# Spreading the routing gates over the adapter rows: eight DMAs inside SBUF in place of eight matmuls with a 0/1 matrix

## The chip, the core and the metric

The kernel runs on one core of a Trainium2 chip. The metric is the device time of one execution in microseconds (us), as the median over several executions. The core has a matrix engine (TensorE, PE in the rows), a vector engine (VectorE, DVE), a scalar engine (ScalarE, ACT), a slower general engine (GpSimd, POOL) and a queue engine that issues most transfers (SyncE, SP). ACT can issue transfers too. Sixteen DMA engines carry all transfers.

## What is computed

The input is a batch of 32 images of 64 rows by 1024 values. Two layers are applied, each as "x plus the feed-forward of a conditioned x". Cut to what matters here:

```
u  = conv1d(x) + context bias                  # layer 0, conditioning
x1 = x + u @ W^T + bias + low-rank adapters    # layer 0, feed-forward
v  = per-image 64x64 mixing of x1 + bias       # layer 1, conditioning

scores = v @ Wr^T                              # 64 scores for each of the 2048 rows
top_vals, top_idx = top_k(scores, 16)
G = 0 everywhere, softmax(top_vals) at top_idx # [2048, 64] gates
h = einsum('nd,krd->nkr', v, A)                # 64 adapters of rank 16: 1024 values a row
out = x1 + 2 * einsum('nkr,kdr->nd', h * G[:, :, None], B)
```

The change is in `h * G[:, :, None]`: one gate of an adapter multiplies the 16 values of its rank.

## The kernel before

**Tiling.** The batch is worked in four groups of 8 images (512 rows each; `g` is the group, `TOK` is 512). Each group goes through the convolution, the first feed-forward, the mixing, the scores, the top 16, `h`, and the last product. The weights come as 24 pieces of 128 x 1024 (`pieces`, 512 KB each) that are loaded anew in every group: pieces 0 to 7 for the first feed-forward, 8 to 15 for `h` (A), 16 to 23 for the last product (B).

**Split products.** Every large product is made of three matmuls of 128x128 by 128x512: the factors are split into a rounded part (`_hi`, made by ACT) and the rest (`_lo`, made by DVE), and `product` (lines 794 to 796) adds hi x hi, lo x hi and hi x lo. So each piece costs ACT one copy (line 390), DVE one subtraction (line 572) and PE 24 matmuls. Three pieces are held at a time (`SLOTS`): a piece is split as soon as the piece three before it has been used (`next_piece` on ACT, `split_piece` on DVE), and SP loads the next one into `raw` when a split is done.

**The stage around the change.** `h` is made in eight chunks of 128 rows (8 adapters x 16 ranks), one for each piece 8 to 15; `h_part(c)` on PE writes chunk `c` to PSUM bank `c % 4`. Beside chunks 1 and 2, DVE finds the 16 largest scores and makes `gate`, laid out by row. PE then turns the gates round (line 951, `banks[6]`: 64 adapters x 512 rows). From there, in the kernel before:

- ACT copies the rounded gates to `gate_r` (line 443), DVE puts the rest beside them (line 699);
- PE multiplies them with `expand_r`, a 0/1 matrix that repeats each adapter's gate on 16 rows (`spread`, line 930), two such matmuls in the middle of each of `h_part(3)` to `h_part(6)`, into banks 7 and 5;
- ACT copies each of these from PSUM to `gate_x` (line 452), which has two slots;
- DVE multiplies chunk `c` of `h` with its slot of `gate_x` into the three-slot `ring` (`gated`, line 708); ACT and DVE split the result into `u_hi` and `u_lo` (lines 405 and 582).

**Who waits for whom.** All order is set by semaphores in code that is written out by hand; each engine works strictly in the order of its own program. `h_part(c)` for `c` from 4 on waits until `gated(c - 4)` has freed its bank (line 914, `s_ring`) and until its piece is split (line 800, `s_piece_lo`). The last product, piece `n` from 16 on, waits for its piece and for the two chunks that it reads (line 967). On DVE the order is: `gated` of two chunks, the two rests `u_lo`, then `split_piece(14)`; the same for the next pairs with pieces 15 and 16; then chunk 6 with piece 17 and chunk 7 with piece 18 (lines 711 to 720).

Of the kernel before, what the change touches and what calls it, by code (L numbers as in the profile page):

```python
# [24 lines left out]
F32 = mybir.dt.float32  # L25
F32R = mybir.dt.float32r
# [5 lines left out]
P = 128  # L32
# [19 lines left out]
RING = 24  # L52
LAG = 3
WARM_UP = 12
NEG = -3.0e38


def adaln_ffn_kernel(nc, conv_x, x, taps, pieces, first_consts, hidden_w, later_consts, lora_a, lora_b,
                     starts, wr, expand, spread, out):
    with ExitStack() as ctx:  # L60
# [22 lines left out]
        mixb_bc = sb("mixb_bc", [P, NB, C])  # L83
        agg = sb("agg", [P, NB // 2, C])
        blockdiag = sb("blockdiag", [P, NT, P])
        expand_r = sb("expand_r", [P, L], F32R)
        lora_a_r = sb("lora_a_r", [P, PH, LORA_M], F32R)
        lora_m1 = sb("lora_m1", [P, L], F32R)
        lora_m2 = sb("lora_m2", [P, L], F32R)
# [9 lines left out]
        expd = sb("expd", [P, NT, KR_E])  # L99
        gate = sb("gate", [P, NT, KR_E])  # L100
        stat = sb("stat", [P, 3, NT])
        gate_r = sb("gate_r", [P, TOK], F32R)
        gate_x = sb("gate_x", [P, 2, TOK])

        consts1 = sb("consts1", [P, sum(w for _, w in FIRST)])
        consts2 = sb("consts2", [P, sum(w for _, w in LATER)])
# [18 lines left out]
        mixb, brow, acol, ecol, mixw = (columns(consts2, LATER, n) for n, _ in LATER)  # L125
        mixw = mixw.rearrange("p (k c) -> p k c", c=C)

        agg_part = gate_x[:, :, :].rearrange("p a (b c) -> p (a b) c", c=C)
        lora_a_raw = score_t[:, 0:PH * LORA].rearrange("p (k m) -> p k m", m=LORA)
        wr_raw = blockdiag[:, :, :].rearrange("p t n -> p (t n)").rearrange("p (k m) -> p k m", m=KR_E)  # L130
        w0s = gate[:, 0:2, :].rearrange("p t e -> p (t e)")
# [3 lines left out]
        reached = left[:, 0, 0:2, :].rearrange("p t e -> p (t e)").rearrange("p (n b) -> p n b", b=NB)  # L135
        count = left[:, 0, 2, :].rearrange("p (n b) -> p n b", b=NB)

        expand_stage, lora_b_stage = x1[:, 0, :], x1[:, 1, :]
        diag = x1[0:C, 2, 0:GB * C].rearrange("p (b c) -> p b c", b=GB)

        banks = [ctx.enter_context(nc.psum_tensor(f"bank{i}", [P, HALF], F32)) for i in range(8)]
# [53 lines left out]
        s_gate = sem("s_gate")  # L195
        s_gate_t = sem("s_gate_t")
        s_gate_hi = sem("s_gate_hi")
        s_gate_lo = sem("s_gate_lo")
        s_spread = sem("s_spread")
        s_gate_x = sem("s_gate_x")  # L200
        s_h = sem("s_h")
        s_out = sem("s_out")
        s_stored = sem("s_stored")
# [28 lines left out]
        @block.sync  # L232
        def _(sp):
            def load_piece(n):
                sp.dma_start(raw[:, n % SLOTS, :], pieces[n % PIECES]).then_inc(s_raw[n % SLOTS], 16)

            def load_conv_in(g, t):
                sp.dma_start(conv_in[:, 2 * t:2 * t + 2].rearrange("p b g q -> p (b g q)"),
                             conv_x[bass.ds(g, 1), t].rearrange("a p n -> (a p) n")).then_inc(s_convin[t], 16)

            def load_x(g, t):
                sp.dma_start(x1[:, t, :], x[bass.ds(g, 1), t].rearrange("a p n -> (a p) n")).then_inc(s_x, 16)

            load_conv_in(0, 0)
            load_taps(sp, 2)
            load_taps(sp, 3)
            sp.dma_start(hidden_stage, hidden_w).then_inc(s_first, 16)
            load_conv_in(0, 1)
            load_piece(0)
            sp.dma_start(consts2[:, :], later_consts).then_inc(s_later, 16)  # L250
            load_conv_in(0, 2)
            load_conv_in(0, 3)
            load_piece(1)
            load_piece(2)
            sp.dma_start(lora_a_raw, lora_a).then_inc(s_expand, 16)
            sp.dma_start(starts_i[:, :], starts.to_broadcast([P, 4])).then_inc(s_starts, 16)
            sp.dma_start(lora_b_stage, lora_b).then_inc(s_expand, 16)
            sp.dma_start(wr_raw, wr).then_inc(s_expand, 16)
            sp.dma_start(expand_stage, expand).then_inc(s_expand, 16)
            def group(g, first, last):  # L260
                for n in range(PIECES):

                    sp.wait_ge(s_piece_lo, g * PIECES + n + 1)
                    load_piece(n + SLOTS)
                    if n == 1 and first:


                        sp.wait_ge(s_const_hi, 5)
                        sp.wait_ge(s_const_lo, 3)
                        sp.wait_ge(s_p_ctx_bc, 1)  # L270
                        for t in range(NT):
                            load_x(0, t)
                    if n == 1 and not last:

                        sp.wait_ge(s_conv, g * GB + GB)
                        for t in range(NT):
                            load_conv_in(g + 1, t)
                    if n == 21:
                        store_half(g, 0)
                store_half(g, 1)  # L280
                if not last:

                    sp.wait_ge(s_stored, g * (16 * 2 * NT) + 16 * 2 * NT)
                    for t in range(NT):
                        load_x(g + 1, t)

            def store_half(g, h):
                for t in range(NT):

                    sp.wait_ge(s_out, g * 8 + 8 + h * NT + t + 1)  # L290
                    sp.dma_start(out[bass.ds(g, 1), t, :, h * HALF:(h + 1) * HALF].rearrange("a p n -> (a p) n"),
                                 x1[:, t, h * HALF:(h + 1) * HALF]).then_inc(s_stored, 16)

            group(0, True, False)
            with sp.Fori(1, GROUPS - 1) as g:
                group(g, False, False)
            group(GROUPS - 1, False, True)
            sp.wait_ge(s_stored, 16 * 2 * NT * GROUPS)
            for n in range(SLOTS):
                sp.wait_ge(s_raw[n], 16 * (GROUPS * PIECES // SLOTS + 1))  # L300
# [35 lines left out]
        def _(act):  # L336
# [29 lines left out]
                               accum_out=attstat[:, 1:2]).then_inc(s_att_exp, 1)  # L366

            def const_hi(n):
                act.wait_ge(s_expand, 64)
                act.wait_ge(s_ones, 4)  # L370
                to, of = ((lora_a_r[:, :, 0:LORA], lora_a_raw), (lora_m1[:, :], lora_b_stage),
                          (lora_m2[0:LORA_LO, :], x1[0:LORA_LO, 1, :]), (wr_r[:, :, 0:KR_E], wr_raw),
                          (expand_r[:, :], expand_stage))[n]
                act.activation(to, of, ACT.Copy).then_inc(s_const_hi, 1)

            def first_after_conv(b):
# [30 lines left out]
            def group(g, first):  # L407
# [5 lines left out]
                    if first:  # L413
                        first_after_conv(b)
                if first:
                    for n in range(5):
                        const_hi(n)
                    biases_out(1, s_mixb, 3, s_out_mixb)
                next_piece(g, 0)
# [18 lines left out]
                for t in range(NT):  # L438
                    act.activation(expd[:, t, :], left[:, 1, t, :], ACT.Exp,
                                   bias=stat[:, 0, t:t + 1]).then_inc(s_exp, 1)  # L440
                next_piece(g, 9)
                act.wait_ge(s_gate_t, g + 1)
                act.activation(gate_r[0:KR_E, :], banks[6][0:KR_E, :], ACT.Copy).then_inc(s_gate_hi, 1)
                next_piece(g, 10)

                def spread(c):

                    act.wait_ge(s_spread, g * NCH + c + 1)
                    if c >= 2:

                        act.wait_ge(s_ring, g * RING + H0 + c - 1)
                    act.activation(gate_x[:, c % 2, :], banks[(7, 5)[c % 2]][:, :], ACT.Copy).then_inc(s_gate_x, 1)

                for c in range(0, NCH, 2):
                    spread(c)
                    spread(c + 1)
                    for k in (c, c + 1):
                        split_hi(g, H0 + k, u_hi[:, k, :], ring[:, (H0 + k) % SLOTS, :])
                        if k != c or c == NCH - 2:
                            next_piece(g, 11 + c // 2 + (k == NCH - 1))  # L460
                for n in range(16, PIECES):
# [7 lines left out]
        def _(dve):  # L469
# [117 lines left out]
            def group(g, first):  # L587
# [103 lines left out]
                for t in range(NT):  # L691
# [2 lines left out]
                                      ALU.mult).then_inc(s_gate, 1)  # L694
                split_piece(g, 11)
                split_piece(g, 12)
                dve.wait_ge(s_gate_t, g + 1)
                dve.wait_ge(s_gate_hi, g + 1)
                dve.tensor_tensor(gate_r[KR_E:P, :], banks[6][0:KR_E, :], gate_r[0:KR_E, :].bitcast(F32),
                                  ALU.subtract).then_inc(s_gate_lo, 1)  # L700
                split_piece(g, 13)

                def gated(c):

                    dve.wait_ge(s_h, g * NCH + c + 1)
                    dve.wait_ge(s_gate_x, g * NCH + c + 1)
                    ring_free(g, H0 + c)
                    dve.tensor_tensor(ring[:, (H0 + c) % SLOTS, :], banks[c % 4][:, :], gate_x[:, c % 2, :],  # L708
                                      ALU.mult).then_inc(s_ring, 1)

                for c in range(0, NCH, 2):
# [26 lines left out]
        def _(pe):  # L738
# [71 lines left out]
            def group(g, first):  # L810
# [110 lines left out]
                    if ks[-1] == NCH - 1:  # L921
                        mm.then_inc(s_h, 1)

                def spread(c):
                    if c == 0:
                        pe.wait_ge(s_gate_hi, g + 1)
                        pe.wait_ge(s_gate_lo, g + 1)
                    if c >= 2:
                        pe.wait_ge(s_gate_x, g * NCH + c - 1)
                    pe.matmul(banks[(7, 5)[c % 2]][:, :], expand_r[:, c * P:(c + 1) * P], gate_r[:, :],  # L930
                              start=True, stop=True).then_inc(s_spread, 1)

                for c in range(NCH + LAG):
                    if c < NCH:
                        mix(c)
# [16 lines left out]
                mm.then_inc(s_gate_t, 1)  # L952
                for c in range(3, NCH):
                    h_part(c, front)
                    if c < 7:
                        spread(2 * (c - 3))
                        spread(2 * (c - 3) + 1)
                    h_part(c, back)


                for n in range(16, PIECES):
                    h, j = (n - 16) // 4, n % 4
                    piece_ready(g, n)
                    if n == 16:
                        pe.wait_ge(s_gate_x, g * NCH + NCH)
                    if h == 0:
                        split_done(g, H0 + 2 * j + 1)
                    for t in range(NT):
# [81 lines left out]
```

## Time and profile before

| what | value |
|---|---|
| median of 3 runs | 718.34 us (718.34 to 720.67) |
| span of the profiled execution | 716.4 us |
| PE busy | 692.5 us, 97% of the span |
| DVE busy | 350.6 us, 49% |
| ACT busy | 202.7 us, 28% |
| POOL busy | 43.8 us, 6% |
| DMA | 81.90 MB, mean 114 GB/s |

The span runs from the first to the last instruction of the profiled execution. The profile gives no other time of that execution; the median of the runs is 1.9 us above the span. Busy time of PE is modelled per matmul, and neighbouring matmuls overlap, so the pace of PE is read from the distance between starts, not from the duration of one.

### The profile page before, as it was taken

The numbers are of one execution on the slowest core, as the hardware profiler recorded it, in microseconds if no ns is written. First come the engines' busy times: TensorE is split into PE (matmuls) and PEld (weight loads), VectorE is DVE, ScalarE is ACT, GpSimd is POOL, SyncE is SP. The second block draws the span as 40 slices with busy tenths as digits, with TensorE's granted clock in tenths as the row PEclk, the third lists the DMA queues.
The fourth block names the chain that finished last, engine by engine and source line by source line (L and its number), as shares of the span: only waits on it lengthen the run. The fifth ranks groups of instructions, "written<-read, shape, count | busy, mean of one in ns | idle before, by whom it ended". The sixth has DMA issues, their size and how long they took to land.

```text
span 716.4 us, 8718 instructions
## 1 busy us (share of the span) xinstructions
PE 692.5 (97%) x3373; PEld 573.9 (80%) x3373; DVE 350.6 (49%) x549; ACT 202.7 (28%) x271; POOL 43.8 (6%) x32
## 2 busy tenths in 40 slices
PE   8955999999999999999999999999999999999998
PEld 7834888888898888888889788888889888888886
DVE  1898356642354327563336335654326333665343
ACT  2611123432122113352222212344112211334211
POOL 1398000000000000000000000000000000000000
PEclk9996999999999999999999999999999999999999
DMA  9156210322446220323427321032245222032342
GB/s 318 66 192 265 89 59 30 118 88 89 147 185 227 67 104 8 100 77 116 148 73 259 137 88 59 29 117 88 88 146 203 96 82 88 6 111 75 101 146 88
DMA packets 25572, 81.90 MB, mean 114 GB/s; under 512 B 3024, under 2 KB 3920, under 8 KB 25424
## 3 DMA queue, kind: packets, MB, share of 16 engines
q1 hardware_dynamic: 24752, 79.36, 32.1%
q10 hardware_dynamic: 800, 2.27, 0.9%
q8 instruction: 13, 0.21, 0.1%
q14 instruction: 7, 0.06, 0.0%
HBM read 73.22 MB, written 8.40 MB: 114 GB/s over the span
## 4 chain that ended last, share of the span: by engine, by line
PE 93%; DVE 5%; DMA 1%; issue 0%; SPq 0%; ACT 0%
PE bank L794 25%; PE bank L796 25%; PE bank L795 25%; PE bank L826 8%; PE bank L893 4%; PE bank L874 2%; PE bank L858 1%; PE bank L856 1%; PE bank L904 1%; PE bank L930 1%; PE bank L903 1%; DVE u_lo L582 1%; DMA gate<-hidden_w 1%; DVE piece_lo L572 1%; DVE left L528 1%
## 5 line engine op out<-in xcount | busy, mean ns | idle before, releaser
L572 DVE TENSOR_TENSOR piece_lo<-raw,piece_hi 128x1024 fp32r<-128x1024 f32 x99 | 126.8, 1286 | 207.3 <-ACT piece_hi L390 207.2
L794 PE MATMUL bank<-piece_hi,u_hi 128*128 128x512 f32 x512 | 203.8, 398 | 15.0 <-DVE piece_lo L572 14.3
L796 PE MATMUL bank<-piece_hi,u_lo 128*128 128x512 f32 x512 | 203.1, 397 | 0.0
L795 PE MATMUL bank<-piece_lo,u_hi 128*128 128x512 f32 x512 | 202.9, 396 | 0.0
L390 ACT ACTIVATE piece_hi<-raw 128x1024 fp32r<-128x1024 f32 x99 | 104.6, 1057 | 305.0 <-PE bank L796 290.6
L794 PEld LDWEIGHTS bank<-piece_hi,u_hi 128*128 128x128 f32 x512 | 97.0, 189 | 39.0 <-DVE piece_lo L572 14.9
L795 PEld LDWEIGHTS bank<-piece_lo,u_hi 128*128 128x128 f32 x512 | 97.0, 189 | 22.9
L796 PEld LDWEIGHTS bank<-piece_hi,u_lo 128*128 128x128 f32 x512 | 96.8, 189 | 23.1
L794 PE MATMUL bank<-v_hi,piece_hi 128*128 128x512 f32 x256 | 101.8, 398 | 0.0
L796 PE MATMUL bank<-v_hi,piece_lo 128*128 128x512 f32 x256 | 101.1, 395 | 0.0
L795 PE MATMUL bank<-v_lo,piece_hi 128*128 128x512 f32 x256 | 100.9, 394 | 0.0
L405 ACT ACTIVATE u_hi<-ring 128x512 fp32r<-128x512 f32 x64 | 40.1, 631 | 73.1 <-DVE ring L708 38.5
L826 PEld LDWEIGHTS bank<-toep,conv_in 128*128 128x128 f32 x512 | 59.4, 195 | 1.5 <-issue 0.8
L826 PE MATMUL bank<-toep,conv_in 128*128 128x128 f32 x512 | 60.3, 280 | 0.0
L796 PEld LDWEIGHTS bank<-v_hi,piece_lo 128*128 128x128 f32 x256 | 48.2, 188 | 11.5
L795 PEld LDWEIGHTS bank<-v_lo,piece_hi 128*128 128x128 f32 x256 | 48.2, 188 | 10.9
L794 PEld LDWEIGHTS bank<-v_hi,piece_hi 128*128 128x128 f32 x256 | 48.2, 188 | 10.9
L582 DVE TENSOR_TENSOR u_lo<-ring,u_hi 128x512 fp32r<-128x512 f32 x64 | 46.2, 733 | 7.1 <-ACT u_hi L405 5.6
L708 DVE TENSOR_TENSOR ring<-bank,gate_x 128x512 f32<-128x512 f32 x32 | 21.4, 689 | 40.0 <-PE bank L796 24.5
L630 DVE TENSOR_TENSOR x<-x,bank 128x512 f32<-128x512 f32 x32 | 22.0, 686 | 25.0 <-PE bank L858 25.0
L893 PEld LDWEIGHTS bank<-blockdiag,x 128*128 128x128 f32 x256 | 31.7, 191 | 1.8
L332 POOL COPY blockdiag<-agg 64x256 f32 x8 | 3.9, 491 | 475.2 <-PE bank L826 474.7
(114 smaller groups left out, 433.8 us busy)
## 6 DMA issues: line engine op xcount, KB each, us to landing
raw<-pieces SPq DMA_DIRECT2D x99, 512.0 KB, 3.3
conv_in<-conv_x SPq DMA_DIRECT2D x16, 516.0 KB, 6.3
x<-x SPq DMA_DIRECT2D x16, 512.0 KB, 5.2
out<-x SPq DMA_DIRECT2D x32, 256.0 KB, 2.4
mixb_bc<-spread ACTq DMA_DIRECT2D x1, 1024.0 KB, 9.2
cond_bc<-spread ACTq DMA_DIRECT2D x1, 768.0 KB, 12.0
x<-lora_b SPq DMA_DIRECT2D x1, 512.0 KB, 10.1
x<-expand SPq DMA_DIRECT2D x1, 512.0 KB, 13.5
```

The source lines that it names most:

```text
L390: act.activation(piece_hi[:, n % SLOTS, :], raw[:, n % SLOTS, :], ACT.Copy).then_inc(s_piece_hi, 1)
L405: act.activation(to, of, ACT.Copy).then_inc(s_hi, 1)
L572: dve.tensor_tensor(piece_lo[:, n % SLOTS, :], raw[:, n % SLOTS, :], piece_hi[:, n % SLOTS, :].bitcast(F32), ALU.subtract).then_inc(s_piec ...
L582: dve.tensor_tensor(to, of, hi, ALU.subtract).then_inc(s_lo, 1)
L630: dve.tensor_tensor(half, half, banks[4 * h + t][:, :], ALU.add).then_inc(s_x1, 1)
L708: dve.tensor_tensor(ring[:, (H0 + c) % SLOTS, :], banks[c % 4][:, :], gate_x[:, c % 2, :], ALU.mult).then_inc(s_ring, 1)
L794: pe.matmul(to, left_hi, right_hi, start=first, stop=False)
L795: pe.matmul(to, left_hi, right_lo, start=False, stop=False)
L796: return pe.matmul(to, left_lo, right_hi, start=False, stop=last)
L826: mm = pe.matmul(banks[4 + b % 4][:, cg * P:(cg + 1) * P], conv_in[:, b, cg, h:h + Q], toep[:, cg, 1 - h, :], start=(h == 0), stop=(h == 1))
L874: mm = pe.matmul(banks[4][0:LORA_M, :], lora_a_r[:, k, :], part[:, k, :], start=(k == 0 and part is u_hi), stop=(k == NCH - 1 and part is ...
L893: mm = pe.matmul(banks[1 + c % 3][:, t * P:(t + 1) * P], x1[:, t, c * P:(c + 1) * P], blockdiag[:, t, :], start=True, stop=True)
```

## The change

The two steps on PE and the hi/rest split of the gates go away. ACT copies the turned gates once, unrounded, to `gate_t` (64 adapters x 512 rows). Then eight DMAs for each group, issued from ACT's queue, copy 8 rows of `gate_t` each to the 128 rows of one slot of `gate_x`, every row 16 times: 8 x 2 KB are read 16 times, 256 KB are written. `gate_x` now has four slots. Four DMAs are issued at once, right behind the copy to `gate_t`; each of the other four is issued by ACT after it has made `u_hi` of the chunk whose slot it takes. The 0/1 matrix, its load of 512 KB and its conversion on ACT go away too.

```diff
+GATES = 4
...
-        expand_r = sb("expand_r", [P, L], F32R)
...
-        gate_r = sb("gate_r", [P, TOK], F32R)
-        gate_x = sb("gate_x", [P, 2, TOK])
+        gate_t = sb("gate_t", [KR_E, TOK])
+        gate_x = sb("gate_x", [P, GATES, TOK])
...
-            sp.dma_start(expand_stage, expand).then_inc(s_expand, 16)
...
-                        sp.wait_ge(s_const_hi, 5)
+                        sp.wait_ge(s_const_hi, 4)
...
-                act.wait_ge(s_expand, 64)
+                act.wait_ge(s_expand, 48)
...
-                    for n in range(5):
+                    for n in range(4):
                         const_hi(n)
...
+                def spread(c):
+
+                    rows = gate_t[c * 8:(c + 1) * 8, None, :].to_broadcast([8, RANK, TOK])
+                    act.dma_start(gate_x[:, c % GATES, :], rows).then_inc(s_gate_x[c % GATES], 16)
+
                 next_piece(g, 9)
                 act.wait_ge(s_gate_t, g + 1)
-                act.activation(gate_r[0:KR_E, :], banks[6][0:KR_E, :], ACT.Copy).then_inc(s_gate_hi, 1)
+                act.activation(gate_t[:, :], banks[6][0:KR_E, :], ACT.Copy).then_inc(s_gate_hi, 1)
+                act.wait_ge(s_gate_hi, g + 1)
+                for c in range(GATES):
+                    spread(c)
                 next_piece(g, 10)
 
-                def spread(c):
-
-                    act.wait_ge(s_spread, g * NCH + c + 1)
-                    if c >= 2:
-
-                        act.wait_ge(s_ring, g * RING + H0 + c - 1)
-                    act.activation(gate_x[:, c % 2, :], banks[(7, 5)[c % 2]][:, :], ACT.Copy).then_inc(s_gate_x, 1)
-
                 for c in range(0, NCH, 2):
-                    spread(c)
-                    spread(c + 1)
                     for k in (c, c + 1):
                         split_hi(g, H0 + k, u_hi[:, k, :], ring[:, (H0 + k) % SLOTS, :])
+                        if k + GATES < NCH:
+
+                            spread(k + GATES)
                         if k != c or c == NCH - 2:
                             next_piece(g, 11 + c // 2 + (k == NCH - 1))
...
-                dve.wait_ge(s_gate_t, g + 1)
-                dve.wait_ge(s_gate_hi, g + 1)
-                dve.tensor_tensor(gate_r[KR_E:P, :], banks[6][0:KR_E, :], gate_r[0:KR_E, :].bitcast(F32),
-                                  ALU.subtract).then_inc(s_gate_lo, 1)
                 split_piece(g, 13)
...
-                    dve.wait_ge(s_gate_x, g * NCH + c + 1)
+                    dve.wait_ge(s_gate_x[c % GATES], g * (16 * NCH // GATES) + 16 * (c // GATES + 1))
                     ring_free(g, H0 + c)
-                    dve.tensor_tensor(ring[:, (H0 + c) % SLOTS, :], banks[c % 4][:, :], gate_x[:, c % 2, :],
+                    dve.tensor_tensor(ring[:, (H0 + c) % SLOTS, :], banks[c % 4][:, :], gate_x[:, c % GATES, :],
                                       ALU.mult).then_inc(s_ring, 1)
...
-                    if c < 7:
-                        spread(2 * (c - 3))
-                        spread(2 * (c - 3) + 1)
                     h_part(c, back)
...
-                        pe.wait_ge(s_gate_x, g * NCH + NCH)
+                        pe.wait_ge(s_gate_hi, g + 1)
```

On PE, the middle of `h_part(3)` in the program of before; L794 to L796 are the three matmuls of one split product, L930 the matmuls with the 0/1 matrix (`gate_r`, `expand_r`):

```order
L795 MATMUL bank<-v_lo,piece_hi 128x512
L796 MATMUL bank<-v_hi,piece_lo 128x512
L930 MATMUL bank<-gate_r,expand_r 128x512 x2
L794 MATMUL bank<-v_hi,piece_hi 128x512
L795 MATMUL bank<-v_lo,piece_hi 128x512
```

On PE in the changed program, from the turning of the gates (L935) into `h_part(3)` (L787 to L789 are the three matmuls of a split product there):

```order
L935 MATMUL bank<-consts,gate 64x128 x4
L787 MATMUL bank<-v_hi,piece_hi 128x512
L788 MATMUL bank<-v_lo,piece_hi 128x512
L789 MATMUL bank<-v_hi,piece_lo 128x512
L787 MATMUL bank<-v_hi,piece_hi 128x512
```

From there on PE has only split products up to the end of the group; the two matmuls in each of four chunks are gone.

On ACT, from the copy of the turned gates on, in the program of before (L452 copies the spread gates out of PSUM, L405 makes `u_hi`, L390 the rounded part of a piece):

```order
L443 ACTIVATE gate_r<-bank 64x512
L390 ACTIVATE piece_hi<-raw 128x1024
L452 ACTIVATE gate_x<-bank 128x512 x2
L405 ACTIVATE u_hi<-ring 128x512 x2
L390 ACTIVATE piece_hi<-raw 128x1024
L452 ACTIVATE gate_x<-bank 128x512 x2
L405 ACTIVATE u_hi<-ring 128x512 x2
L390 ACTIVATE piece_hi<-raw 128x1024
```

The same stretch on ACT in the changed program (L440 is the issue of a DMA from `gate_t` to `gate_x`, L401 makes `u_hi`, L386 the rounded part of a piece):

```order
L444 ACTIVATE gate_t<-bank 64x512
L440 DMA gate_x<-gate_t 128x1x512 x4
L386 ACTIVATE piece_hi<-raw 128x1024
L401 ACTIVATE u_hi<-ring 128x512
L440 DMA gate_x<-gate_t 128x1x512
L401 ACTIVATE u_hi<-ring 128x512
L440 DMA gate_x<-gate_t 128x1x512
L386 ACTIVATE piece_hi<-raw 128x1024
```

ACT's copies into `gate_x` are replaced by DMA issues; four of them stand ahead of the split of piece 13, the others stand between `u_hi` of a chunk and what follows.

## Rows read from the trace of the kernel before

**Rows 1.** Page, parts 1 and 4: busy times, and shares of the chain that ended last.

```profile
PE 692.5 (97%) x3373; PEld 573.9 (80%) x3373; DVE 350.6 (49%) x549; ACT 202.7 (28%) x271; POOL 43.8 (6%) x32
...
PE 93%; DVE 5%; DMA 1%; issue 0%; SPq 0%; ACT 0%
```

**Rows 2.** Waits over the span: engine, line, releaser, us in total, times, longest.

```profile
DVE ring L708 <- PE bank L796: 24.5, 12, 2.5
...
DVE ring L708 <- ACT gate_x L452: 15.5, 12, 1.5
PEld bank L794 <- DVE piece_lo L572: 14.9, 2, 13.4
PE bank L794 <- DVE piece_lo L572: 14.3, 2, 13.0
```

**Rows 3.** Groups of instructions by line and shape: matmuls with the 0/1 matrix.

```profile
L930 PE MATMUL bank<-gate_r,expand_r 128*128 128x512 f32 x32 | 10.0, 394 | 0.0
```

**Rows 4.** Chain that ended last, 145 to 160 us: start, us, what.

```profile
151.19 0.23 PE bank L796
151.43 0.46 PE bank L930 x2
152.81 0.23 PE bank L795
```

**Rows 5.** Timeline of ACT, 115 to 190 us: start, us, engine, line, op.

```profile
130.53 0.59 ACT L443 ACTIVATE gate_r<-bank 64x512 fp32r<-64x512 f32 x1 [4.95 <-PE bank L951]
...
165.90 1.06 ACT L390 ACTIVATE piece_hi<-raw 128x1024 fp32r<-128x1024 f32 x1 [3.29 <-PE bank L796]
171.50 1.06 ACT L390 ACTIVATE piece_hi<-raw 128x1024 fp32r<-128x1024 f32 x1 [4.54 <-PE bank L796]
```

**Rows 6.** Timeline of DVE, 115 to 190 us.

```profile
148.67 0.69 DVE L708 TENSOR_TENSOR ring<-bank,gate_x 128x512 f32<-128x512 f32 x1 [1.64 <-PE bank L796]
149.28 1.48 DVE L582 TENSOR_TENSOR u_lo<-ring,u_hi 128x512 fp32r<-128x512 f32 x2
151.01 1.23 DVE L572 TENSOR_TENSOR piece_lo<-raw,piece_hi 128x1024 fp32r<-128x1024 f32 x1 [0.26 <-ACT piece_hi L390]
```

**Rows 7.** Timeline of ACT, 28 to 70 us: the conversion of the matrix, then issues.

```profile
32.94 1.04 ACT L374 ACTIVATE expand_r<-x 128x1024 fp32r<-128x1024 f32 x1
45.16 0.31 ACTq L355 DMA_DIRECT2D spread<-biases  x1
...
48.47 0.47 ACTq L360 DMA_DIRECT2D cond_bc<-spread  x1
```

**Rows 8.** DMA issues by line: count, KB each, median us to landing.

```profile
raw<-pieces SPq DMA_DIRECT2D x99, 512.0 KB, 3.3
...
out<-x SPq DMA_DIRECT2D x32, 256.0 KB, 2.4
...
x<-expand SPq DMA_DIRECT2D x1, 512.0 KB, 13.5
```

**Rows 9.** Windows of 5 us: busy of each engine, PEclk, DMA share, GB/s.

```profile
50.00:55.00 5.00, 0.00 (x0) 0.00 (x0) 4.90 (x5) 0.09 (x1) 4.84 (x3) 0.89 1.02 414
55.00:60.00 5.00, 0.00 (x0) 0.00 (x0) 4.86 (x5) 0.00 (x0) 4.84 (x3) 0.50 1.01 410
```

**Rows 10.** Waits of SP's queue over the span.

```profile
SPq L270 <- DVE wr_r L546: 7.5, 1, 7.5
```

**Rows 11.** Chain that ended last, up to 80 us: matmuls behind the long stop.

```profile
63.28 0.43 PE bank L796
...
68.07 0.24 PE bank L796
```

More of the change, by code:

```diff
@@ L126, in adaln_ffn_kernel @@
         mixw = mixw.rearrange("p (k c) -> p k c", c=C)
-        agg_part = gate_x[:, :, :].rearrange("p a (b c) -> p (a b) c", c=C)
+        agg_part = gate_x[:, 0:2, :].rearrange("p a (b c) -> p (a b) c", c=C)
         lora_a_raw = score_t[:, 0:PH * LORA].rearrange("p (k m) -> p k m", m=LORA)
@@ L136, in adaln_ffn_kernel @@
         count = left[:, 0, 2, :].rearrange("p (n b) -> p n b", b=NB)
-        expand_stage, lora_b_stage = x1[:, 0, :], x1[:, 1, :]
+        lora_b_stage = x1[:, 1, :]
         diag = x1[0:C, 2, 0:GB * C].rearrange("p (b c) -> p b c", b=GB)
@@ L197, in adaln_ffn_kernel @@
         s_gate_hi = sem("s_gate_hi")
-        s_gate_lo = sem("s_gate_lo")
-        s_spread = sem("s_spread")
-        s_gate_x = sem("s_gate_x")
+        s_gate_x = [sem(f"s_gate_x{n}") for n in range(GATES)]
         s_h = sem("s_h")
@@ L368, in const_hi @@
             def const_hi(n):
-                act.wait_ge(s_expand, 64)
+                act.wait_ge(s_expand, 48)
                 act.wait_ge(s_ones, 4)
                 to, of = ((lora_a_r[:, :, 0:LORA], lora_a_raw), (lora_m1[:, :], lora_b_stage),
-                          (lora_m2[0:LORA_LO, :], x1[0:LORA_LO, 1, :]), (wr_r[:, :, 0:KR_E], wr_raw),
-                          (expand_r[:, :], expand_stage))[n]
+                          (lora_m2[0:LORA_LO, :], x1[0:LORA_LO, 1, :]), (wr_r[:, :, 0:KR_E], wr_raw))[n]
                 act.activation(to, of, ACT.Copy).then_inc(s_const_hi, 1)
@@ L922, in h_part @@
                         mm.then_inc(s_h, 1)
[L924 to L931, printed above, removed]
                 for c in range(NCH + LAG):
```

## The prediction

> **What bounds the kernel now.** First the busy times and the chain that ended last [rows 1]: PE is busy for 97% of the span and holds 93% of the chain, while DVE and ACT stand at 49% and 28%. So a matmul that goes is worth its full time, and a wait of PE that comes costs its full time. Then the waits [rows 2]: PE stood still for 14.3 us behind DVE's piece split, 13.0 of them in one stop, in group 0; no wait of PE names the spreading of the gates. DVE did wait for ACT's copies of the gates (15.5 us) and for `h` (24.5 us), both off PE's path. The stage around the change thus has no gap on PE, and I work it out in group 0, the four groups running the same code there.
>
> **The pace of PE.** ACT splits one piece each time PE has used one, so the starts of ACT's splits in the last product, 165.90 and 171.50 [rows 5], are 5.60 us apart: 24 matmuls at 0.233 us. I call this a unit. Two matmuls with the 0/1 matrix take 0.46 us in the chain [rows 4], the same pace; the 394 ns of their group [rows 3] are overlapping durations.
>
> **What is removed.** There are 32 such matmuls [rows 3] at 0.233 us: **-7.5 us**, all of it on PE's path. ACT's copies to `gate_x` and DVE's subtraction for `gate_r` go too, on engines that are not the bound: 0. The 512 KB load of the matrix is the last of the first batch that SP issues, it landed after 13.5 us [rows 8], and nothing stood behind it; its conversion, 1.04 us at 32.94 [rows 7], came well ahead of the 45 us at which ACT issued the next thing, and the loads of `x` that wait for the constants waited for DVE's `wr_r`, not for ACT [rows 10]: 0. If that cover were gone it would be 1.04 us. The long stop in group 0 is DVE's own chain of constants and stays.
>
> **What is added: the issues.** An issue holds ACT for 0.31 to 0.47 us [rows 7]; I take 0.43. Four stand ahead of the split of piece 13, 1.7 us; that piece is wanted two units after the gates are turned, so they are hidden, as are the single issues later, but for one (below). If the split of piece 13 had no slack, it would be 1.7 us a group.
>
> **What is added: the wait for the data.** `gated(0)` needs the first DMA's data, and `h_part(4)` needs `gated(0)`. Let d be the time that one DMA takes out of a queue of them, and F the fixed part from issue to landing. In the trace all 16 engines together moved 414 GB/s [rows 9], 25.9 GB/s for each. A store of 256 KB from SBUF lands after 2.4 us [rows 8]; at 414 GB/s its data take 0.6, so F = 1.8 us. (A piece, 512 KB, would need 1.8 + 1.3 = 3.1, and has 3.3.)
>
> For d the trace has no like: every large transfer in it touches all 128 partitions of SBUF, while here all 256 KB come out of 8. The lower bound is 0.6 us, all engines at their rate. The upper bound comes from the same 414 GB/s: an even sixteenth of SBUF, 8 partitions, was never seen to pass more than 25.9 GB/s, which makes d = 10.1 us. Eight partitions next to each other need not be served together, though: they can belong to two such groups or more. I take two, d = 5.06 us, since the row that resembles the read most is the rate at which a set of 8 partitions was served, and every further group is a guess in the change's favour. This is the choice on which the forecast hangs.
>
> The Trainium skill weighs on it too (SBUF — State Buffer, Door 1: the DMA port swizzle): 128 partitions hang on 16 ports, four neighbours to a port, so 8 consecutive partitions reach only two, at about 27 GB/s each. By that page d would be 4.8 us as an estimate; no run here shows it yet. A second rule (DMA: Bandwidth & Descriptors, Why a DMA increments its semaphore by 16 and not by 1) speaks against the change as well: a source whose slowest dimension is 8 is carried by 8 of the 16 engines. That alone would change little, as the second rival shows.
>
> **The sum in one group.** The gates are turned at 130.5; ACT's copy ends at 131.1 [rows 5]; the first issue is done at 131.5. The DMAs are queued, so slot data c land at 131.5 + (c + 1)d + 1.8, which holds up to c = 5 when d is long, since the fifth and sixth are issued before the fourth is through. PE begins `h_part(3)` at 130.35 and, with nothing between the units, wants `h_part(4)` at 135.95, `h_part(7)` at 152.75 and piece 16 at 158.35. Against that:
> - `h_part(4)`: landing 138.4, then the product 0.69 [rows 6] and 0.1 to PE: 139.2, **3.2 us** late.
> - `h_part(7)` needs piece 15, which DVE splits behind `gated(3)`. From the start of the second product of such a pair to the end of the piece's split took 148.67 to 152.24, 3.57 us [rows 6]; one issue on ACT lies in between, 0.43: 4.0. Landing 153.5 + 4.0 = 157.5, against 152.75 + 3.2 = 156.0: **1.5 us**.
> - Piece 16 stands behind `gated(5)`: landing 163.7 + 3.6 = 167.3, against 158.35 + 4.7 = 163.1: **4.2 us**.
> - Chunks 6 and 7 with pieces 17 and 18 land 5.1 us apart, less than a unit: 0.
>
> That is 8.9 us a group, in short 6d - 21.45, and 35.8 over four groups. The stops are followed by work at PE's full pace and nothing gives them back. The sum: 718.3 - 7.5 + 35.8 = **746.6 us**, against the median; on the span, 744.7. In the stops PE's neighbours are late in turn: DVE and ACT, which wait for the landing, and SP's loads, which wait for DVE's splits.
>
> **The turning point.** Only the first stop is left when d is under 3.9: d - 1.85. It eats the 1.9 us of matmuls that a group saves at d = 3.7 us, 71 GB/s out of eight partitions. Slower than this the change loses, faster it wins.
>
> **The rivals.**
> 1. **Rows at two groups' rate**, as summed: 746.6. Chance 0.56. Its own range, 735 to 760: d from 4.6 (17 us net) to 5.6, where the loads of pieces, 32 KB for each engine in every unit, get in between (41 us net).
> 2. **Each engine at its own rate, hidden** (the other side: faster). If eight engines take a row each and the source sets no limit, d = 32 KB / 25.9 GB/s = 1.3 us. The first landing is at 134.6, the product is done at 135.3, before the 135.95: no stop. 718.3 - 7.5 = **710.9 us**. For it: no row shows SBUF itself as the limit of a transfer, and the store, which reads 256 KB from it, lands in 2.4 us. Against it: the store reads from all partitions, and no row has so few of them as a source. Chance 0.31.
> 3. **In between**, d from 2.2 to 4: stops of 0.4 to 2.6 us a group, 712 to 721. Chance 0.09, split over faster, same and slower as 0.03, 0.04, 0.02.
> 4. **One group's rate**, d = 10.1: 6d - 21.45 = 39 us a group, and pieces 17 and 18 then come 10.1 - 5.6 = 4.5 us late each as well: 48 us a group, 718.3 - 7.5 + 192 = 903. For it only that it is the bound. Chance 0.04.
> A cost on top, in cases 1 and 4: in the long stop PE did nothing from 50 to 55 us, at a mean granted clock of 0.89, and nothing from 55 to 60, at 0.50, the lower level of 1.2 GHz [rows 9]; behind it matmuls took 0.43 instead of 0.23 us [rows 11]. The stops summed here are shorter than the first of these windows, so I count nothing for the clock; with it case 1 would pass 760.
>
> **Numbers.** The likeliest case gives 746.6. The range has to hold case 2 (710.9, less the 1 to 2 us by which my pace or a hidden cost can be off) and case 1 up to d = 5.5: 709 to 758. Outside lie case 4 and the upper edge of case 1. What a measurement of this kernel can tell from no change is about 0.5%, 3.6 us, that is 714.7 to 721.9. Faster: 0.31 + 0.03 = 0.34; same: 0.04, with 0.01 for case 1 running into it: 0.05; slower: 0.61.
>
> **What the profile of the changed kernel would show.** The landing time of `gate_x<-gate_t`: near 7 us for the first and over 15 for the fourth in case 1, under 4 in case 2. PE waiting for `ring` and for `piece_lo` in 12 stops, near 9 us a group, in case 1; none but the old ones in case 2. DVE's products with a DMA as releaser. The rest as before: the stop in group 0, the unit of 5.60 us, and 32 matmuls fewer. The prediction is wrong if the eight rows come out at over 71 GB/s, or if the DMAs overlap so that four land in the time of one or two.

## The result, and the profile after

The changed kernel takes **751.33 us** (median of 6 runs, 749.87 to 755.29), the kernel before, beside it, 720.04 us (718.34 to 722.01). The ratio is 1.0445, with a 95% interval of 1.0422 to 1.0469: slower by 31.3 us, where 28.3 were forecast. One execution of the kernel before, beside the later experiments, took 866.17 us at a mean granted clock of 0.747 and is left out of every comparison. The time lies in the range; the way there is another one than the prediction's, as its profile shows at once.

The page of the changed kernel, the rows that answer to [rows 1] and [rows 8]:

```profile
span 748.3 us, 8615 instructions
...
PE 692.2 (93%) x3341; PEld 571.5 (76%) x3341; DVE 347.4 (46%) x545; ACT 185.0 (25%) x238; POOL 43.8 (6%) x32
...
PEclk9987999799999999989999999989999999998999
...
PE 86%; DMA 7%; DVE 5%; issue 1%; ACT 0%; ACTq 0%; SPq 0%; DVEq 0%
...
gate_x<-gate_t ACTq DMA_DIRECT2D x32, 256.0 KB
```

The row of the granted clock on the page of the kernel before:

```profile
PEclk9996999999999999999999999999999999999999
```

The chain that ended last now holds 7% of DMA, and the granted clock has dips (an 8 or a 7) once in each group, which the kernel before had not; its one dip, the 6, is the long stop in group 0. The waits of the changed kernel, beside [rows 2] (engine, line, releaser, us in total, times, longest):

```profile
DVE piece_lo L569 <- ACT piece_hi L386: 278.3, 78, 14.4
ACT piece_hi L386 <- issue: 60.3, 13, 10.1
...
PE bank L787 <- DVE ring L701: 32.5, 4, 8.2
...
PE bank L787 <- DVE piece_lo L569: 14.3, 2, 12.9
```

PE has one new stop in each group, four times about 8.1 us, not three. And ACT stands still in "issue", 10.1 us at the longest: it waits for nothing but its own issuing. The timeline of ACT in group 0, beside [rows 5]:

```profile
129.25 0.59 ACT L444 ACTIVATE gate_t<-bank 64x512 f32<-64x512 f32 x1 [4.95 <-PE bank L935]
129.88 9.83 ACTq L440 DMA_DIRECT2D gate_x<-gate_t  x4
139.81 1.06 ACT L386 ACTIVATE piece_hi<-raw 128x1024 fp32r<-128x1024 f32 x1 [9.97 <-issue]
142.76 0.63 ACT L401 ACTIVATE u_hi<-ring 128x512 fp32r<-128x512 f32 x1 [1.89 <-DVE ring L701]
```

The four issues take 9.83 us; I had taken 4 x 0.43. Only then is piece 13 rounded. DVE in the same stretch:

```profile
140.90 1.23 DVE L569 TENSOR_TENSOR piece_lo<-raw,piece_hi 128x1024 fp32r<-128x1024 f32 x1 [14.33 <-ACT piece_hi L386]
142.05 1.28 DVE L701 TENSOR_TENSOR ring<-bank,gate_x 128x512 f32<-128x512 f32 x2
```

DVE's program has the split of piece 13 ahead of the first product with the gates. It stood 14.33 us for ACT's rounding, and made the product only after that, at 142.05. The windows of 1 us show what PE and the DMA engines did meanwhile (busy of each engine, then PEclk, DMA share, GB/s):

```profile
134.00:135.00 1.00, 0.82 (x4) 0.34 (x2) 0.00 (x0) 0.00 (x0) 0.00 (x0) 1.00 0.46 49
135.00:136.00 1.00, 0.00 (x0) 0.00 (x0) 0.00 (x0) 0.00 (x0) 0.00 (x0) 1.00 0.45 47
136.00:137.00 1.00, 0.00 (x0) 0.00 (x0) 0.00 (x0) 0.00 (x0) 0.00 (x0) 0.86 0.47 86
137.00:138.00 1.00, 0.00 (x0) 0.00 (x0) 0.00 (x0) 0.00 (x0) 0.00 (x0) 0.50 0.48 51
```

Nothing but the spreading is in flight from 131 to 142 us. While one DMA is being served it brings 47 to 51 GB/s, at a share of 0.45 to 0.48: about half of the sixteen engines are busy. 256 KB at 49 GB/s are 5.35 us, where I had taken 5.06. In the window 136 to 137, where slot 0's DMA ends and slot 1's begins, it is 86 GB/s, and from 140 to 142, where slot 1's ends, 96 and 107: two of these DMAs that overlap bring more together than one. PE stops at 134.8; the granted clock is still 1.00 from 135 to 136, 0.86 in the next window and 0.50 from 137 on (1.2 in place of 2.4 GHz).

When the data land isn't among the profile's rows for this DMA; the semaphores' own events, read from the same trace for group 0, give it:

```
slot  issue begins  issue takes  last part landed
0     129.88        0.67         136.94
1     130.59        0.62         141.49
2     131.24        4.18         145.66
3     135.45        4.26         149.49
```

So slot 0 was there at 136.94, 7.06 us behind its issue and 5.1 us before DVE used it. The first two issues pass at once; the third and fourth take 4.2 us each, about the distance between two landings (4.6, 4.2 and 3.8 us).

### The profile page after: what moved, and what is told of

Its sections match the earlier page's. It is cut to its first block, busy times and chain, and to the rows that moved or that the text cites. A ratio compares the mean times of both kernels' runs of the same rounds, so it can differ in the third digit from the quotient of the medians.

```text
span 748.3 us, 8615 instructions
## 1 busy us (share of the span) xinstructions
PE 692.2 (93%) x3341; PEld 571.5 (76%) x3341; DVE 347.4 (46%) x545; ACT 185.0 (25%) x238; POOL 43.8 (6%) x32
## 4 chain that ended last, share of the span: by engine, by line
PE 86%; DMA 7%; DVE 5%; issue 1%; ACT 0%; ACTq 0%; SPq 0%; DVEq 0%
PE bank L787 23%; PE bank L788 23%; PE bank L789 23%; PE bank L819 7%; DMA gate_x<-gate_t 6%; PE bank L886 4%; PE bank L867 1%; PE bank L851 1%; PE bank L849 1%; PE bank L897 1%; PE bank L896 1%; DVE u_lo L579 1%; DMA gate<-hidden_w 1%; DVE piece_lo L569 1%; DVE left L525 1%
## 5 line engine op out<-in xcount | busy, mean ns | idle before, releaser
L787 PE MATMUL bank<-piece_hi,u_hi 128*128 128x512 f32 x512 | 203.5, 397 | 15.0 <-DVE piece_lo L569 14.3
L789 PE MATMUL bank<-piece_hi,u_lo 128*128 128x512 f32 x512 | 202.6, 396 | 0.0
L386 ACT ACTIVATE piece_hi<-raw 128x1024 fp32r<-128x1024 f32 x99 | 104.7, 1058 | 360.2 <-PE bank L789 286.9
L787 PE MATMUL bank<-v_hi,piece_hi 128*128 128x512 f32 x256 | 105.3, 411 | 32.5 <-DVE ring L701 32.5
L787 PEld LDWEIGHTS bank<-piece_hi,u_hi 128*128 128x128 f32 x512 | 96.8, 189 | 39.0 <-DVE piece_lo L569 14.9
L789 PEld LDWEIGHTS bank<-piece_hi,u_lo 128*128 128x128 f32 x512 | 96.6, 189 | 23.0
L788 PE MATMUL bank<-v_lo,piece_hi 128*128 128x512 f32 x256 | 103.8, 405 | 0.0
L789 PE MATMUL bank<-v_hi,piece_lo 128*128 128x512 f32 x256 | 103.3, 403 | 0.0
L787 PEld LDWEIGHTS bank<-v_hi,piece_hi 128*128 128x128 f32 x256 | 50.0, 195 | 45.5 <-DVE piece_lo L569 34.1
L401 ACT ACTIVATE u_hi<-ring 128x512 fp32r<-128x512 f32 x64 | 40.3, 631 | 92.1 <-DVE ring L701 56.7
L789 PEld LDWEIGHTS bank<-v_hi,piece_lo 128*128 128x128 f32 x256 | 49.8, 195 | 12.2
L788 PEld LDWEIGHTS bank<-v_lo,piece_hi 128*128 128x128 f32 x256 | 49.9, 195 | 11.3
L886 PE MATMUL bank<-blockdiag,x 128*128 128x128 f32 x256 | 31.8, 275 | 0.0
## 6 DMA issues: line engine op xcount, KB each, us to landing
cond_bc<-spread ACTq DMA_DIRECT2D x1, 768.0 KB, 12.2
```

The lines of the kernel that those rows point to most:

```text
L386: act.activation(piece_hi[:, n % SLOTS, :], raw[:, n % SLOTS, :], ACT.Copy).then_inc(s_piece_hi, 1)
L401: act.activation(to, of, ACT.Copy).then_inc(s_hi, 1)
L787: pe.matmul(to, left_hi, right_hi, start=first, stop=False)
L788: pe.matmul(to, left_hi, right_lo, start=False, stop=False)
L789: return pe.matmul(to, left_lo, right_hi, start=False, stop=last)
L886: mm = pe.matmul(banks[1 + c % 3][:, t * P:(t + 1) * P], x1[:, t, c * P:(c + 1) * P], blockdiag[:, t, :], start=True, stop=True)
```

## The experiments

The theory after this profile, **A, the hold**: the stop is set by ACT, held by its issues, through piece 13 and DVE's order. Its rival, **B, the landing**: the first products wait for the data, as the chain of waits says, which names the DMA from 130.59 for 10.90 us. And for the rate, **C**: neighbouring rows share one way out of SBUF, against **D**: an engine that reads one row sixteen times, or eight engines, can do no more. The kernel before ran at 718.4 us beside the first four and at 719.1 us beside the others.

**DVE's order turned** (`dve_order`): the split of piece 13 behind the first product.

```diff
                 split_piece(g, 12)
-                split_piece(g, 13)
...
                         if c < NCH - 2:
                             gated(k)
+                        if k == 0:
+                            split_piece(g, 13)
```

> The changed kernel with one line moved on DVE: the split of piece 13 stands behind the first product of a chunk with its gates instead of ahead of it. ACT still issues four DMAs before it rounds piece 13. Theory A (the hold): PE's stop of 8.1 us a group ahead of h_part(4) is there because ACT is held for 9.8 us by the four issues, so that piece 13 is rounded late, and DVE, which splits it before the first product, is held with it; the first DMA's data have long landed (about 137 us in group 0). Then the stop shrinks to the landing, 3.1 us a group, the clock does not fall, and the time is about 725 to 728 us. Theory B (the landing): the first products wait for data that land at 141.5 us, as the chain that ended last names the DMA; then nothing changes, 751 us.

Measured: 732.0 us, 1.0194 (1.0177 to 1.0211). Moving one line takes 18 of the changed kernel's 31 us of loss away; 13.6 us are left against the kernel before beside it. The first product now follows the landing; timeline of DVE, and of ACT:

```profile
138.37 0.69 DVE L700 TENSOR_TENSOR ring<-bank,gate_x 128x512 f32<-128x512 f32 x1 [10.43 <-issue]
142.35 1.22 DVE L569 TENSOR_TENSOR piece_lo<-raw,piece_hi 128x1024 fp32r<-128x1024 f32 x1 [3.29 <-ACT piece_hi L386]
```

```profile
131.25 9.91 ACTq L440 DMA_DIRECT2D gate_x<-gate_t  x4
```

7.1 us from the first issue to the product instead of 12.2; the hold is as long as ever, but nobody on PE's path waits behind it. PE's waits for `ring` fall from 32.5 to 13.0 us. Theory B falls. The time is 4 to 7 us over what I expected: PE's stop was 3.0 to 3.1 us in every group, as expected, but I had the clock stay up, and it fell behind some of these stops too (below).

**ACT's order turned** (`act_order`): piece 13 rounded ahead of the issues.

```diff
+                next_piece(g, 10)
                 act.wait_ge(s_gate_hi, g + 1)
                 for c in range(GATES):
                     spread(c)
-                next_piece(g, 10)
```

> The changed kernel with ACT's order turned: piece 13 is rounded before the four DMAs are issued, so the issues and all landings come 1.1 us later. Theory A: piece 13 no longer waits for the hold; the stop of PE is the landing of the first DMA, 1.1 us later than in the run with DVE's order turned: 4.1 us a group, about 728 to 732 us. Theory B: the landing is the limit and comes 1.1 us later: 755 us.

Measured: 730.7 us, 1.0174 (1.0131 to 1.0217). The time is the one that A expected, but not by its sum. The issues did not come later: ACT's copy of the gates starts at 131.05 and the first issue at 131.67, 0.62 us later as in `dve_order`, while ACT rounds piece 13 from 131.54 on. So PE's stop is 3.3 to 3.4 us a group and not 4.1, and the rest is the clock. Theory B falls here too. The clock behind two stops of nearly the same length, group 0 of `dve_order` (3.0 us), then of `act_order` (3.3 us):

```profile
140.00:146.00 6.00, 6.00 (x21) 4.70 (x21) 2.49 (x4) 2.21 (x3) 0.00 (x0) 0.74 0.58 121
```

```profile
140.00:146.00 6.00, 6.00 (x26) 4.89 (x27) 1.29 (x2) 1.22 (x2) 0.00 (x0) 1.00 0.48 108
```

At a mean granted clock of 0.74 PE starts 21 matmuls in the 6 us, at 1.00 it starts 26.

**Issued from SP** (`sp_issue`): the same DMAs from the other queue; ACT issues none of them.

```diff
                     load_piece(n + SLOTS)
+                    if n == 12:
+                        sp.wait_ge(s_gate_hi, g + 1)
+                    for c in {12: (0, 1, 2, 3), 14: (4, 5), 15: (6, 7)}.get(n, ()):
+                        if c >= GATES:
+                            sp.wait_ge(s_ring, g * RING + H0 + c - GATES + 1)
+                        rows = gate_t[c * 8:(c + 1) * 8, None, :].to_broadcast([8, RANK, TOK])
+                        sp.dma_start(gate_x[:, c % GATES, :], rows).then_inc(s_gate_x[c % GATES], 16)
```

> The changed kernel with the same eight DMAs issued from SP's queue instead of ACT's, four behind the load that follows the split of piece 12, two each behind those of pieces 14 and 15. ACT is not held at all. Theory A: the first landing stays at about 7 us behind the gates, the stop is 3.1 us a group, about 725 us, and the hold shows up on SP's queue (about 10 us for four issues). Theory B: 751 us.

Measured: 731.7 us, 1.0178 (1.0155 to 1.0201), some 7 us over the expectation. The hold moves with the issues, as SP's timeline shows; it belongs to these DMAs and not to ACT:

```profile
132.25 9.86 SPq L268 DMA_DIRECT2D gate_x<-gate_t  x4
```

**Rows at a distance of 8** (`rows_by_eights`): other source rows, and the host's layout of A and B to match.

```diff
-                    rows = gate_t[c * 8:(c + 1) * 8, None, :].to_broadcast([8, RANK, TOK])
+                    rows = gate_t[c:KR_E:NCH, None, :].to_broadcast([8, RANK, TOK])
```

> The changed kernel with another distribution of the adapters over the chunks: each DMA reads the rows c, c+8, ... c+56 of the gates instead of eight neighbours (the rows of both weight arrays are laid out on the host to match; the result is the same). Engines, bytes, packets and program order stay. Theory C (shared way out of SBUF): neighbouring rows share it, so a DMA comes at 49 GB/s; eight rows at a distance of 8 lie on twice as many, about 100 GB/s, 2.6 us a DMA; the first lands about 4.5 us behind its issue, the hold on ACT halves to about 5 us, PE's stop is about 3 us, 724 to 727 us. Theory D (each engine reads one row sixteen times, and that is what is slow, or eight engines give no more): unchanged, 49 GB/s and 751 us.

Measured: 735.7 us, 1.0242 (1.0218 to 1.0265). The rate doubles, with the same share of the engines (windows of 1 us), and the hold shrinks (timeline of ACT):

```profile
134.00:135.00 1.00, 1.00 (x6) 0.82 (x5) 0.00 (x0) 0.00 (x0) 0.00 (x0) 1.00 0.49 106
135.00:136.00 1.00, 1.00 (x6) 0.82 (x5) 0.00 (x0) 0.00 (x0) 0.00 (x0) 1.00 0.49 100
```

```profile
132.72 5.66 ACTq L440 DMA_DIRECT2D gate_x<-gate_t  x4
138.48 1.06 ACT L386 ACTIVATE piece_hi<-raw 128x1024 fp32r<-128x1024 f32 x1 [5.80 <-PE bank L789]
```

The first DMA lands 4.46 us behind its issue, where C had 4.5. C holds and D falls: the limit of 49 GB/s lies in which rows are read, not in the engines, the packets or the repeated reads. What it is that neighbouring rows share, the runs don't show. The Trainium skill's map (SBUF — State Buffer, Door 1: the DMA port swizzle) agrees: eight neighbours lie on two ports, rows at a distance of 8 on four.

The time was 9 to 12 us over the expectation: PE's wait for `ring` was 3.9 us in each group instead of 3, since piece 13 still came late through ACT and DVE, and the clock fell in all four groups (0.72 in the window 140 to 146).

**Both mended** (`both_mended`): rows at a distance of 8, and DVE's order turned.

> The rows at a distance of 8 and DVE's order turned, together; ACT's order as in the changed kernel. Each mended one of two limits and was then held by the other: with neighbouring rows the first landing came 7 us behind the issue, with rows at a distance 4.5 us, but piece 13 came late. Theory A and C together: the stop is the landing, 4.5 us behind the first issue, product 0.7, so 0.7 to 1 us a group, too short for the clock: 718.4 - 7.5 + 4 = about 715 us. If ACT's hold of 5 to 6 us shows up again (u_hi of the first chunk or piece 13 late for h_part(5)), up to 720 us.

Measured: 714.0 us, 0.9933 (0.9910 to 0.9956): the change, mended in two places, is faster than the kernel before, by 5.1 us or 0.7%. PE's waits for `ring` are 1.8 us in all (0.5 at the longest), and the clock stays up:

```profile
134.00:140.00 6.00, 5.53 (x24) 4.20 (x23) 0.69 (x1) 0.55 (x1) 0.00 (x0) 1.00 0.42 87
```

**The stop filled** (`filled_stop`): what the clock costs by itself.

```diff
                     h_part(c, back)
+                    if c == 3:
+                        for _ in range(30):
+                            pe.matmul(banks[7][:, :], wr_r[:, 0, :], v_hi[:, 0, :], start=True, stop=True)
```

> The changed kernel with 30 matmuls more in each group, 7.0 us of them, behind h_part(3), where PE stops for 8.1 us; their result goes to a PSUM bank that nobody reads. They change neither the landings nor ACT's hold. If the clock is a cost of its own (behind the stop some ten matmuls take 0.43 us instead of 0.23), PE stays at full clock and the time falls by 1.5 to 2 us a group, to 743 to 745 us, the stop itself, 8.1 us a group, being filled and not removed. If the clock costs nothing beyond the stop, it stays at 751 us.

Measured: 747.0 us, 1.0391 (1.0364 to 1.0419), where the changed kernel has 1.0445 (1.0422 to 1.0469). More work on PE, and less time: 4.3 us by the medians, 3.4 us when each is taken against the kernel before beside it, 6.8 us by the profiled spans (741.5 against 748.3). That is about 1 us a group by the medians, less than the 1.5 to 2 that I expected. The stop is where it was, and PE was busy in it at full clock:

```profile
134.00:140.00 6.00, 6.00 (x28) 4.92 (x27) 0.00 (x0) 0.00 (x0) 0.00 (x0) 1.00 0.47 58
```

**One DMA for all chunks** (`one_dma`). Each chunk of `h` takes two ranks of all 64 adapters instead of sixteen ranks of eight; only the host's layout of A and B changes. The spread gates are then the same for all eight chunks.

```diff
-                for c in range(GATES):
-                    spread(c)
+                act.dma_start(gate_x[:, 0, :], gate_t[:, None, :].to_broadcast([KR_E, 2, TOK])).then_inc(s_gate_x[0], 16)
...
+    def two_ranks(m):
+        return np.asarray(m).reshape(KR_E, NCH, 2, L).transpose(1, 0, 2, 3)
```

> The adapters are laid out over the chunks in another way: every chunk holds all 64 adapters with two of their ranks, so all eight chunks need the same spread gates, and one DMA a group from all 64 rows of the gates (each read twice) replaces eight. Theory C: 64 rows have eight ways out instead of two, some 200 GB/s, about 1.3 us and 1.8 fixed; it lands 3 to 3.5 us behind its issue, one issue doesn't hold ACT, no stop: 718.4 - 7.5 = 711 us. Rival: the landing has a floor that keeps the stop, over 4.2 us from issue to landing: 715 us or more.

Measured: 711.4 us, 0.9902 (0.9875 to 0.9929). The page has the landing time:

```profile
gate_x<-gate_t ACTq DMA_DIRECT2D x4, 256.0 KB, 3.0
```

The same 256 KB out of 64 rows land after 3.0 us, instead of 7.06 out of 8, and no wait of PE for `ring` is left.

**No spreading at all** (`no_spread`): the same layout; DVE writes every gate twice, PE turns the gates to 128 rows.

```diff
-                    mm = pe.transpose(banks[6][0:KR_E, t * P:(t + 1) * P], gate[:, t, :], ident)
+                    mm = pe.transpose(banks[6][:, t * P:(t + 1) * P], gate2[:, t, :], ident)
...
-                act.activation(gate_t[:, :], banks[6][0:KR_E, :], ACT.Copy).then_inc(s_gate_hi, 1)
+                act.activation(gate_x[:, 0, :], banks[6][:, :], ACT.Copy).then_inc(s_gate_hi, 1)
```

> The same layout of the chunks, and no spreading at all: DVE writes each gate twice (128 columns instead of 64), PE turns them to 128 rows at once, ACT copies that once to gate_x, and DVE uses it for all eight chunks. Neither the 32 matmuls nor any DMA between SBUF and SBUF are left. It measures what the 32 matmuls are worth: 718.4 - 7.5 = 711 us, less or more by what the wider turn costs (16 weight loads of 128 instead of 64 columns, under 1.5 us). If the matmuls had been hidden behind something else it would stay near 718 us.

Measured: 711.7 us, 0.9904 (0.9882 to 0.9925), 7.4 us under the kernel before; PE is busy for 684.8 us in place of 692.5. The 32 matmuls were worth their 7.5 us. It can't be told from `one_dma`; both beat the kernel before and the changed one.

## Why the prediction was right, and where it was not

- **The bound and the saving.** Right: PE is the bound, and the matmuls are worth 0.233 us each. `no_spread` is 7.4 us under the kernel before by medians, -7.5 was the sum.
- **The data rate d.** Right in size: 49 GB/s, d = 5.35 us alone and 4.6, 4.2 and 3.8 us between the later landings, against 5.06. The first landing came 7.06 us behind its issue (expected near 7), the fourth 14.0 us behind its own (expected over 15). The DMAs overlap a little, so the fourth was through at 149.5; the sum's 153.5 would be 152.2 here, since the gates are turned 1.3 us earlier in this trace. The bound from [rows 9], taken twice, was a choice; `rows_by_eights` shows that the choice was of the right kind, since twice the spread of the rows gives twice the rate.
- **The issues: the step that failed.** "An issue holds ACT for 0.31 to 0.47 us; I take 0.43. Four stand ahead of the split of piece 13, 1.7 us ... so they are hidden." They took 9.83 us. [rows 7] showed issues with at most one other DMA of ACT's queue in flight, and of the gates' DMAs too the first two go out in 0.6 us each. It is the third that waits for the drain, so a run of slow transfers holds its issuer. In `sp_issue`, where ACT issued none of them, its hold was gone and SP had it. I had priced the slowness only where its data are waited for.
- **What is queued behind it.** The split of piece 13 stands on DVE ahead of the first product. I worked out the landing against `h_part(4)` and left that line out, so my first stop of 3.2 us was 8.1. With that one line moved (`dve_order`) the stop is 3.0 to 3.1 us: the landing was right, the path to it was not.
- **The other two stops** (1.5 and 4.2 us) did not come: everything behind the first stop was already 8.1 us late, and the later landings were nearer to each other than d. The second reason counts by itself: in `dve_order`, with a first stop of 3.1 us, what came behind it was 0 in the first two groups and at most 1.5 us in the last. Sum of my three: 8.9; the one measured: 8.1. (Four times 8.9 is 35.6, not 35.8.)
- **The clock.** I counted nothing for stops shorter than 5 us. It fell in each group. The span shows 31.9 more; 32.5 of waits for `ring` less 7.5 of matmuls leave 6.9 us, 1.7 a group. The windows of 1 us behind the four stops agree: PE's busy time times what the granted clock lacked of 1.00 adds up to 7.5 us; in `filled_stop` it is 0. `filled_stop` gives 4.3 us by medians. That the total came out within 5 us of the forecast is luck, errors that cancel: a step at 0.43 us that took up to 4.26, one stop for three, and the clock on top.
- **What the runs with one mend show together.** Each single mend leaves PE 12.1 to 15.5 us of waits for `ring` and a ratio of about 1.02; both together leave 1.8 us. 718.4 - 7.5 and those waits make 723 to 726 us, where 731 to 736 were measured: 6 to 9 us more. The clock is the greater part of it where it can be read. The stops of one kernel are alike in all four groups, yet it fell behind one of them in `dve_order`, two in `act_order`, three in `sp_issue` and all four in `rows_by_eights`; read from windows of 1 us as above, that costs 1.7, 4.7, 6.4 and 8.1 us in the profiled executions. The span before (716.4), less 7.5, with the waits and this clock comes to 723.6, 727.0, 727.4 and 732.5 us, where the profiled spans are 726.4, 728.0, 729.7 and 734.3; those last 1 to 3 us stay open. The profiled execution of `dve_order` was its fastest, 728.2 us against a median of 732.0, and had the highest mean granted clock of the five, 0.984 where the others had 0.972 to 0.979.

## What to carry to other kernels

Price a DMA inside SBUF by the rows it reads, not by its bytes: eight neighbouring rows gave 49 GB/s, eight spread ones 100 to 106, and 256 KB out of 64 rows landed in 3.0 us. Several slow DMAs in a row can hold the engine that issues them, here from the third one on, so look at what stands behind the issue on that engine, and at what the engines that it feeds do in order. And before making a step faster, ask whether its layout needs it: with two ranks of every adapter in a chunk, eight spreadings became one or none.

## What the runs showed of the hardware that was not expected

- **The issue waits for the drain.** Two issues of 0.6 us, then 4.2 us each, from ACT (9.83 us for four) and from SP (9.86); 5.66 us when the rows are spread and each DMA drains in half the time, with the same number of packets. It is no rule of two for every DMA: at the start of the changed kernel SP issued 15 loads from 0.7 to 9.4 us, each in 0.39 to 0.83 us, though the last four of them landed 9.7 us and more behind their issue. What of the gates' DMAs brings the hold was not tried.
- **About half of the DMA engines** (share 0.47 to 0.51) serve a DMA whose source begins with a dimension of 8. The Trainium skill (DMA: Bandwidth & Descriptors, Why a DMA increments its semaphore by 16 and not by 1) gives eight engines for it; the trace agrees. It was not the limit here, since the rate doubled on as many engines.
- **Short stops can bring the clock down, and equal stops need not do the same.** PE stood from 134.8; the granted clock was 1.00 in the window 135 to 136, 0.86 in the next and 0.50 after it. Stops of 3.0 to 3.1 us were followed by a lower clock in one group of four (`dve_order`) and in three of four (`sp_issue`), stops of 3.3 to 3.4 us in two of four (`act_order`), stops of 3.9 and 8.1 us in all four (`rows_by_eights`, the changed kernel), stops of 0.5 us in none (`both_mended`).
